# A ring of four square buffers and interleaved halves in the statistics of the last layer norm

## What is computed

```
a   = conv1d(x, 3 taps, 4096 -> 3*1024) -> q, k, v -> causal attention in blocks of 128
x1  = layernorm(x + proj(attention))            # over the 4096 features, eps 1e-5
y   = x1 + x1 @ W.T + b + low-rank experts(x1)  # 4096 -> 4096
out = layernorm(y)                              # (y - mean) / sqrt(var + eps)
```

## Time and profile before

| | us |
|---|---|
| median of 3 runs | 2419.72 |
| the profiled execution | 2420.2 |
| its span, first to last instruction, slowest core (core 1) | 2418.7 |
| spans of the 8 cores | 2404.8 to 2418.7 |
| first square of the LN2 statistics starts | 2208.45 |
| last square of them starts | 2303.01 |
| the first chain starts reading the banks | 2304.52 |

### The profile page before, as it was taken

One profiled execution on the slowest core, in us unless ns is written; L12 is line 12 of the kernel. 1 busy time (PEld: TensorE's weight loads), 2 busy tenths in 40 slices (PEclk: granted clock), 3 DMA queues, 4 the chain that ended last, 5 costly groups with the idle time before them and its releaser, 6 DMA issues.

```text
span 2418.7 us, 20421 instructions; the slowest of 8 cores (2404.8 to 2418.7 us)
## 1 busy us (share of the span) xinstructions
PE 1939.2 (80%) x8762; PEld 835.7 (35%) x8762; DVE 231.3 (10%) x158; ACT 301.9 (12%) x413; POOL 409.4 (17%) x364
## 2 busy tenths in 40 slices
PE   0399999999999999999826666572799999998600
PEld 0144444444444444444312222221344444442000
DVE  0000000000000000000421003006000000000078
ACT  0000000000000000003055333140000000002410
POOL 1112121211212121200001211216000000000068
PEclk9999999999999999999858888896899999997555
DMA  9988989898989979742205675766155555550034
GB/s 143 94 73 75 90 74 89 74 87 79 86 84 79 86 69 86 66 42 35 35 1 73 78 94 68 98 78 70 35 70 70 70 70 70 70 70 0 0 117 161
DMA packets 436620, 176.12 MB, mean 73 GB/s; under 512 B 301875, under 2 KB 420787, under 8 KB 436276
## 3 DMA queue, kind: packets, MB, share of 16 engines
q0 software_dynamic: 425728, 157.32, 61.8%
q1 hardware_dynamic: 10804, 17.50, 2.0%
HBM read 315.32 MB, written 16.78 MB: 137 GB/s over the span
## 4 chain that ended last, share of the span: by engine, by line
PE 72%; DMA 10%; POOL 5%; issue 5%; ACT 4%; DVE 3%; ACTq 0%; POOLq 0%; DVEq 0%
PE psB L335 21%; PE psA L335 19%; PE psA L1039 18%; DMA xjb<-xT 7%; DMA cwb<-cw 2%; POOL ob L1102 2%; POOL ob L1098 2%; ACT sqtmp L997 2%; PE psB L1015 2%; PE psA L922 1%; PE psA L795 1%; PE psA L689 1%; PE psA L392 1%; PE psA L1049 1%; PE psB L392 1%
## 5 line engine op out<-in xcount | busy, mean ns | idle before, releaser
L335 PE MATMUL psA<-xb,cwb 128*128 128x512 bf16 x2304 | 501.1, 379 | 100.8 <-DMA cwb<-cw 100.7
L335 PE MATMUL psB<-xb,cwb 128*128 128x512 bf16 x2304 | 499.2, 378 | 0.3 <-DMA cwb<-cw 0.3
L335 PEld LDWEIGHTS psA<-xb,cwb 128*128 128x128 bf16 x2304 | 223.4, 97 | 377.4 <-issue 104.2
L335 PEld LDWEIGHTS psB<-xb,cwb 128*128 128x128 bf16 x2304 | 223.0, 97 | 275.5 <-issue 1.3
L298 POOL DMA_DIRECT2D cwb<-cw x144 | 164.8, 1175 | 845.6 <-PE psA L335 416.2
L1039 PE MATMUL psA<-x1bA,wsF 128*128 128x512 bf16 x1024 | 227.8, 381 | 15.4 <-DMA Bmb<-Bm 15.4
L1039 PEld LDWEIGHTS psA<-x1bA,wsF 128*128 128x128 bf16 x1024 | 100.5, 98 | 137.6 <-issue 18.0
L1039 PE MATMUL psA<-x1bB_lo,wsF 128*128 128x512 bf16 x512 | 115.7, 379 | 0.0
L1039 PE MATMUL psA<-x1bB_hi,wsF 128*128 128x512 bf16 x512 | 115.7, 379 | 0.0
L951 POOL DMA_DIRECT2D wsF<-Wt x16 | 26.8, 1678 | 459.4 <-PE psA L1057 370.6
L804 PE MATMUL psA<-xjb,idb 128*128 128x512 bf16 x64 | 28.8, 450 | 89.8 <-DMA xjb<-xT 89.7
(11 more groups left out here) (152 smaller groups left out, 1243.7 us busy)
## 6 DMA issues: line engine op xcount, KB each, us to landing
cwb<-cw POOLq DMA_DIRECT2D x144, 512.0 KB, 23.0
wsF<-Wt POOLq DMA_DIRECT2D x16, 2048.0 KB, 18.8
outT<-ob SPq DMA_DIRECT2D x64, 256.0 KB, 2.2
xb<-xT POOLq DMA_DIRECT2D x4, 2052.0 KB, 44.5
wsA<-projw POOLq DMA_DIRECT2D x16, 512.0 KB, 6.4
wsB<-projw POOLq DMA_DIRECT2D x16, 512.0 KB, 6.2
xjb<-xT POOLq DMA_DIRECT2D x64, 128.0 KB, 5.6
wqpre<-wq POOLq DMA_DIRECT2D x8, 256.0 KB, 35.1
```

The lines of the kernel that those rows point to most:

```text
L335: return e.matmul(pbank(bank), buf[:, (w * 32 + dc) * 128:(w * 32 + dc + 1) * 128], xb[:, dc * (T + 2) + tokc * 512 + w: dc * (T + 2) + to ...
```

## The change

Three buffers are laid over the region `REG1`, which held the FFN's weight stream and is free when the FFN's last matmul has finished: `sq4`, four tiles of 512 bf16 columns, and two tiles of 512 f32 columns for the second chain. The squares of LN2 go to tile `(2 * oc + half) % 4` of `sq4`; a square waits for the mm2 that last read this tile, which is that of four calls before, and for the FFN's end. The loop goes through the chunks outside and the halves inside. The chain of half 1 gets its own two temporaries. Lines of the changed kernel have other numbers: 997 becomes 1002, 1006 becomes 1012, 1015 becomes 1021.

```
+    sq4 = sb("sq4", REG1, (128, 2048), BF16)
+    l2tmp1 = sb("l2tmp1", REG1 + 8192, (128, TH), F32)
+    l2tmp2 = sb("l2tmp2", REG1 + 10240, (128, TH), F32)
...
-    def emit_ln_chain(st, nm_t, rstd_t, make_bf=False):
+    def emit_ln_chain(st, nm_t, rstd_t, make_bf=False, tmps=None):
+        t1_, t2_ = tmps if tmps else (tmp1, tmp2)
...
     def emit_stats2(oc, half, c_evac):
         hs = ln2[half]
+        slot = (2 * oc + half) % 4
...
-                sqtmp[:, half * 512:half * 512 + 512],
+                sq4[:, slot * 512:slot * 512 + 512],
                 res2_ap(oc)[:, half * TH:half * TH + TH], AF.Square)
-        sqw = [("cC", c_evac)]
-        if oc >= 1:
-            sqw.append(("tC", hs["mm2_done"][oc - 1]))
+        sqw = [("cC", c_evac), t_ffn_end]
+        prev = stats2_slot_tc.get(slot)
+        if prev is not None:
+            sqw.append(("tC", prev))
...
+        stats2_slot_tc[slot] = S.n("tC")
...
-    for half in range(2):
-        for oc in range(DC):
+    t_ffn_end = ("tC", S.n("tC"))
+    for oc in range(DC):
+        for half in range(2):
             emit_stats2(oc, half, res2_writes[(oc, half)])
...
         gate = emit_ln_chain(st, nm_t, rs_t, make_bf=False,
+                             tmps=None if half == 0 else (l2tmp1, l2tmp2))
```

More of the change, by code:

```diff
@@ L871, in emit_ln_chain @@
             wait=cw_)
[L872 to L875, removed]
+        S.op("scalar", lambda e, t1_=t1_: e.activation(
+            t1_[:, :], pbank(b1), AF.Square, bias=0.0, scale=1.0 / D))
+        S.op("scalar", lambda e, t2_=t2_: e.activation(
+            t2_[:, :], pbank(b2), AF.Copy, bias=1e-5, scale=1.0 / D))
         c_st = S.n("cC")
@@ L878, in emit_ln_chain @@
         bank_free[b2] = ("cC", c_st)
-        S.op("vector", lambda e: e.tensor_sub(tmp2[:, :], tmp2[:, :],
-                                              tmp1[:, :]),
-             wait=[("cC", c_st)])
+        S.op("vector", lambda e, t1_=t1_, t2_=t2_: e.tensor_sub(
+            t2_[:, :], t2_[:, :], t1_[:, :]), wait=[("cC", c_st)])
         v_r = S.n("vC")
[L883 to L886, removed]
+        S.op("scalar", lambda e, t1_=t1_, t2_=t2_: e.activation(
+            t1_[:, :], t2_[:, :], AF.Ln), wait=[("vC", v_r)])
+        S.op("scalar", lambda e, rs_out=rs_out, t1_=t1_: e.activation(
+            rs_out[:, :], t1_[:, :], AF.Exp, bias=0.0, scale=-0.5))
         return ("cC", S.n("cC"))
@@ L992, in build_nc, with sq2 @@
     res2_writes = {}
+    stats2_slot_tc = {}
     def emit_stats2(oc, half, c_evac):
         hs = ln2[half]
-        def sq2(e, oc=oc, half=half):
+        slot = (2 * oc + half) % 4
+        def sq2(e, oc=oc, half=half, slot=slot):
             return e.activation(
-                sqtmp[:, half * 512:half * 512 + 512],
+                sq4[:, slot * 512:slot * 512 + 512],
                 res2_ap(oc)[:, half * TH:half * TH + TH], AF.Square)
-        sqw = [("cC", c_evac)]
-        if oc >= 1:
-            sqw.append(("tC", hs["mm2_done"][oc - 1]))
+        sqw = [("cC", c_evac), t_ffn_end]
+        prev = stats2_slot_tc.get(slot)
+        if prev is not None:
+            sqw.append(("tC", prev))
         S.op("scalar", sq2, wait=sqw)
@@ L1013, in emit_stats2, with mm2 @@
         hs["w"][hs["b1"]] = []
-        def mm2(e, oc=oc, half=half, b2=hs["b2"]):
+        def mm2(e, oc=oc, half=half, b2=hs["b2"], slot=slot):
             return e.matmul(
                 pbank(b2), ones128[:, :],
-                sqtmp[:, half * 512:half * 512 + 512],
+                sq4[:, slot * 512:slot * 512 + 512],
                 start=(oc == 0), stop=(oc == DC - 1),
@@ L1085, in build_nc @@
         rs_t = rstd if half == 0 else rstd2
-        gate = emit_ln_chain(st, nm_t, rs_t, make_bf=False)
+        gate = emit_ln_chain(st, nm_t, rs_t, make_bf=False,
+                             tmps=None if half == 0 else (l2tmp1, l2tmp2))
         apply_specs.append((half, nm_t, rs_t, gate))
```

## The result

The changed kernel takes 2373.13 us (median of 10 runs, 2366.95 to 2568.24), against 2421.64 us for the kernel before (10 runs, 2417.26 to 2578.15). The ratio is 0.9791, 95% interval 0.9776 to 0.9806, and the medians are 2370.8 (six runs, 2366.95 to 2374.55) and 2421.4 (nine runs). The profiled execution took 2369.96 us, its span on the slowest core (now core 6) 2368.4.

What follows compares the result with a forecast made beforehand. The ACT-PE round trip in LN2's statistics, neither engine itself, was taken as the bound. 2420.2 - 49.1 (statistics) - 0.2 (last leg) = 2370.9, or 2370.4 from the runs' median; 2370.5 taken, range 2367 to 2375.

Steps and rivals of the forecast that it cites:

- The wait that goes: LN2 statistics: the return from mm2 to the next square, in a turn of 1.50 us, disappears; 49.1 us saved.
- What is late next: LN2 statistics: ACT's pace of 0.721 us a step at high clock, or PE's 0.85 at low clock.
- squares end to end: LN2 squares on ACT: a step of 0.63 us instead of 0.72 would give 2365 us; chance 2%.
- I expect the clock to fall here again: Start of LN2 statistics: PE's clock falls after the first idle time, which remains after the change.
- a low stretch makes PE full: LN2 statistics: at 1.2 GHz PE needs 0.85 us every 0.72; high clock returns, four tiles give 1.37 us slack.
- The last leg: LN2, last square to first read of the banks: 1.31 us instead of 1.51, 0.2 us saved.
- The temporaries and the FFN wait: Second chain's own temporaries and the squares' wait for the FFN's end: 0 gained, 0 lost; the chains' 8.9 us remain.
- The apply: Stage after the chains, bound by DVE and POOL: moves earlier as a block, priced at 0, between -0.5 and +2 us.
- The low clock for most of the stage: LN2 statistics: PE's clock falls repeatedly or never rises; 8.3 us at full price, giving 2379 us; chance 8%.
- PSUM banks: LN2 statistics: four open banks make each matmul drain, a turn of 1.26 us, giving 2405 us; chance 2%.
- The ring that does not decouple: LN2 statistics: ACT and PE stay in turns for another reason than the tile, 1.50 us stays, 2420; chance 2%.
- the slower case: LN2 statistics: serial turns also take in mm1, 2.0 us a turn, 31 us more, giving 2452 us; chance 2%.

Runs made afterwards that it cites:

- the ring alone: Kernel before with four square tiles instead of two, all chunks of half 0 still before half 1: 2370.48 us, ratio 0.9789.
- the interleaving alone: Kernel before with halves inside the chunk loop, keeping the old two tiles, one for each half: 2370.77 us, ratio 0.9795.
- The experiment with DVE: Changed kernel with the squares of half 1 moved from ACT to DVE as tensor multiplies: 2356.62 and 2357.21 us, ratio 0.9731.
- the cold start: Twelve dummy ACT squares before the statistics, added to the changed kernel: 2378.18 us; added to interleaved halves with two tiles: 2380.67 us.

## Why the prediction was right

Predicted 2370.5, measured 2370.8. That they agree to 0.3 us is in part luck: the six runs lie between 2366.95 and 2374.55, and the kernel before took 2421.4 here and not the 2419.72 that the sum started from, so the medians differ by 50.6 us where the stage gives 49.3. What is shown is the stage, to a tenth of a microsecond.

- **The wait that goes.** Right. The 62 waits for mm2 are gone, and the first square to the last takes 45.4 us as summed. That the tile was its cause is shown: the ring alone and the interleaving alone each remove it. The prediction took the turn of 1.50 us as it stood. Some of it was the clock's: on core 4 of the kernel before, the first turns ran at the high level and took 1.30 each. So of the 0.78 us by which a turn got shorter, about 0.20 is the clock's, 12 to 13 us of the 49 as an estimate (63 x 0.20). It comes only where the new turns keep the clock high, as they did here.

```profile
2204.40 0.38 PE L1015 MATMUL psB<-sqtmp,ones_s 128*128 128x512 bf16 x1 [1.49 <-ACT sqtmp L997]
...
2205.70 0.38 PE L1015 MATMUL psB<-sqtmp,ones_s 128*128 128x512 bf16 x1 [0.71 <-ACT sqtmp L997]
...
2208.31 0.38 PE L1015 MATMUL psB<-sqtmp,ones_s 128*128 128x512 bf16 x1 [0.71 <-ACT sqtmp L997]
...
2209.61 0.59 PE L1015 MATMUL psB<-sqtmp,ones_s 128*128 128x512 bf16 x1 [0.70 <-ACT sqtmp L997]
```

- **What is late next.** Right: ACT at 0.721 a step, now for 64 squares in a run. The experiment with DVE shows that ACT was the bound and PE at 0.43 a pair comes next.
- **Why ACT's step is 0.721.** The prediction took the row and left the reason at "fits". The reason is shown now: without the self-wait the step is 0.520. The bound "squares end to end", 0.63, wasn't a bound at all, since squares overlap; for the changed kernel, which keeps the self-wait, it didn't matter.
- **The clock.** The step "I expect the clock to fall here again" failed on five of eight cores: it stayed at 1.00 through the same first idle time of 1.49 us that stood before the fall in the earlier trace rows. It held on cores 1, 2 and 3. In the kernel before, the clock fell on all eight, but only behind one to four more idle times of 0.71 us (core 4 above has four), and these the changed kernel doesn't have. So the idle time of 1.49 us, which the step went by, didn't decide it alone; what does is open. The other part, that a low stretch makes PE full, gives way to the high clock, and is absorbed by the ring, was right, on these three cores and in the cold start on all eight. So the sum had nothing riding on the part that failed.
- **The last leg** 1.3 us instead of 1.51, as summed. **The temporaries and the FFN wait** 0, as priced. **The apply** 102.8 us in both.
- **The rivals.** The low clock for most of the stage, and with it the oscillation that the Trainium skill describes in "TensorE: Matmul & The Clock Gate" (a second HAM failure mode): not seen; the clock was 1.00 for the 37 us of the body while PE had idle time in every turn and changed bank at every matmul. PSUM banks: the ring alone has two open and the same step. The ring that does not decouple, and the slower case: not seen.

What differs from the sum outside the stage is small: core 6 finished its FFN 0.9 us earlier in its execution than core 1 in that of before, and the span fell by 50.3 where the stage accounts for 49.3. Cores differ by more than that: in the changed kernel's profiled execution the first square starts between 2193.8 and 2207.6.

## What to carry to other kernels

When two engines each show about half busy and each waits for the other, look for the buffer that closes the circle: here one tile, and a distance of two calls between uses was enough. Price the fix from another place in the same trace that runs the same instructions with the distance you will have; it gives the next bound too. Then ask whether the stage has to stand alone: spread over the matmul stage before it, the same work cost 0.44 us a tile instead of 0.72, and a wait of each instruction for its predecessor is worth a look wherever an engine is the bound.

## What the runs showed that I had not expected

ACT squares of 512 bf16 columns with immediate operands, each lasting 0.62 to 0.63 us, started every 0.520 us once they no longer waited for one another, and every 0.721 with the wait. The granted clock stayed at its high level through 1.49 us of idle PE on five cores, and fell soon after it on three: the same instructions don't decide it. In the kernel before, PE was busy for 53.80 of 80 us at the low clock and stayed there; in the changed one it is busy for 29.92 of 37 us at the high clock and stays there.
